# Self-attention's front in a decoder block: the order of its DMAs, its scaling and latent products, and one gather on another engine

## The reference

```python
x = _layernorm(x + ffn0)                                   # per entry of the batch
ct_q  = x @ Wd_q_w + Wd_q_b;  ct_kv = x @ Wd_kv_w + Wd_kv_b    # the latents, 64 wide each
query = heads(ct_q @ Wu_q_w + Wu_q_b) + heads(_rope(ct_q @ Wq_r_w + Wq_r_b, cos, sin))
key   = heads(ct_kv @ Wu_k_w + Wu_k_b) + heads(_rope(x @ Wk_r_w + Wk_r_b, cos, sin))
value = heads(ct_kv @ Wu_v_w + Wu_v_b)                     # 16 heads, 8 wide
attn  = softmax(einsum('bhqd,bhkd->bhqk', query, key) / 12)
out   = einsum('bhqk,bhkd->bhqd', attn, value) @ Wo_w + Wo_b
```

## Time and profile before

| | us |
|---|---|
| median of 3 runs (lowest to highest) | 450.51 (449.87 to 451.18) |
| the profiled execution's own time | 447.8 |
| its span, first to last instruction | 446.0 |
| TensorE busy in the span | 407.5 (91%) |
| VectorE busy | 303.2 (68%) |
| ScalarE busy | 205.1 (46%) |
| GpSimd busy | 196.5 (44%) |
| mean granted clock, as a share of 2.4 GHz | 0.986 |

### The profile page before, as it was taken

How to read it: one execution, slowest core, us unless ns; L and a number is a source line. 1 busy time by engine, 2 the same in 40 slices (tenths; PEclk the granted TensorE clock), 3 DMA queues, 4 the chain that set the end, 5 groups by cost and what they waited for, 6 DMA issues and landing times.

```text
span 446.0 us, 7698 instructions
## 1 busy us (share of the span) xinstructions
PE 407.5 (91%) x2882; PEld 275.8 (62%) x2882; DVE 303.2 (68%) x688; ACT 205.1 (46%) x290; POOL 196.5 (44%) x237
## 2 busy tenths in 40 slices
PE   4898999999999999989999986799779999999985
PEld 4576644455555557747898764445555555558974
DVE  4779976768988888624424978573798894355654
ACT  1676633154333333242333476457256545557550
POOL 3316657699988887050322556212453233000000
PEclk9989999999999999999999998899999999999999
DMA  8812000000005111350251015100000000010000
GB/s 299 320 33 85 2 1 1 1 1 0 1 0 190 48 47 48 100 193 1 103 77 22 2 31 69 15 3 3 0 2 3 2 3 2 2 37 1 0 1 24
DMA packets 8080, 19.78 MB, mean 44 GB/s; under 512 B 1958, under 2 KB 3974, under 8 KB 7526
## 3 DMA queue, kind: packets, MB, share of 16 engines
q1 hardware_dynamic: 8044, 19.30, 14.6%
HBM read 17.26 MB, written 1.15 MB: 41 GB/s over the span
## 4 chain that ended last, share of the span: by engine, by line
PE 72%; DVE 14%; DMA 5%; issue 3%; POOL 3%; ACT 3%; SPq 0%; DVEq 0%; POOLq 0%; ACTq 0%
PE ps L1676 70%; DMA late<-mid 4%; DVE ps L1421 3%; DVE big L1227 2%; DVE ps L1222 2%; DVE mx_a L1425 1%; PE ps L1688 1%; DMA ident<-in_ident 1%; DVE big L1298 1%; POOL rstd L638 1%; POOL big L657 1%; PE ps L2150 1%; PE ps L2073 0%; ACT late L1073 0%; DVE mid L1451 0%
## 5 line engine op out<-in xcount | busy, mean ns | idle before, releaser
L1676 PE MATMUL ps<-big,late 128*32 128x256 f32 (+3 forms) x768 | 96.1, 380 | 3.2 <-DVE mx_a L1425 1.5
L967 ACT ACTIVATE big<-ps 128x1024 f32<-128x1024 f32 x48 | 49.0, 1023 | 39.5 <-PE ps L1676 39.3
L1676 PE MATMUL ps<-late,big 128*128 128x128 f32 (+1 forms) x448 | 65.6, 277 | 1.5 <-DMA late<-mid 1.5
L1676 PEld LDWEIGHTS ps<-big,late 128*32 128x32 f32 (+2 forms) x768 | 36.7, 116 | 38.1 <-issue 14.9
L1676 PEld LDWEIGHTS ps<-late,big 128*128 128x128 f32 (+1 forms) x448 | 47.2, 152 | 19.7 <-issue 12.9
L636 POOL TENSOR_SCALAR vareps<-meanvar 128x2 f32<-128x2 f32 (+2 forms) x13 | 2.9, 226 | 110.0 <-DVE meanvar L1121 106.2
L907 ACT ACTIVATE big<-ps 128x1024 f32<-128x1024 f32 x32 | 31.0, 1022 | 38.9 <-PE ps L1676 37.5
L1421 DVE CUSTOM_DVE_ANT_0 ps<-ps,big 128x512 f32<-128x512 f32 x64 | 42.7, 708 | 6.9 <-PE ps L1676 5.8
L703 POOL TENSOR_TENSOR big<-big 128x512 f32<-128x512 f32 x31 | 43.8, 1428 | 5.5 <-DVE big L1298 5.3
L1298 DVE TENSOR_SCALAR big<-big 128x1024 f32<-128x1024 f32 x32 | 36.4, 1159 | 13.2 <-ACT big L907 12.8
L929 ACT ACTIVATE big<-ps 128x512 f32<-128x512 f32 x32 | 19.1, 597 | 36.7 <-PE ps L1676 36.7
(11 more groups left out here) (261 smaller groups left out, 754.4 us busy)
## 6 DMA issues: line engine op xcount, KB each, us to landing
attn_w<-in_w_x SPq DMA_DIRECT2D x1, 2560.0 KB, 13.6
big<-parts_kx SPq DMA_DIRECT2D x18, 128.0 KB
late<-in_w_up SPq DMA_DIRECT2D x1, 2048.0 KB, 7.8
late<-in_w_dn SPq DMA_DIRECT2D x4, 512.0 KB, 3.8
attn_w<-in_w_up SPq DMA_DIRECT2D x1, 1024.0 KB, 7.9
attn_w<-in_w_dn SPq DMA_DIRECT2D x1, 1024.0 KB, 10.1
big<-mid SPq DMA_DIRECT2D x24, 32.0 KB, 1.8
parts_kx<-ctx_r SPq DMA_DIRECT2D x1, 768.0 KB, 3.2
```

The costliest lines, as they stand in the source:

```text
L967: nc.scalar.activation(ex1[:, n % 3, :].rearrange("p (r n) -> p r n", r=2), ps[:, 2 * (n % 2):2 * (n % 2) + 2, :], ACT.Exp, scale=scale).t ...
L1676: return nc.tensor.matmul(o, lhsT, rhs, start=start, stop=stop, skip_group_check=shared)
```

## The change

It edits only the order and the place of instructions.

- One query gather, `("qa", 1, 1)`, moves from GpSimd to VectorE, which does it right behind its gather `("qa", 1, 0)`.
- `stack_x` can issue some of its pieces. SP now issues the maxima of group 0 first, then six pieces of half 0, the maxima of group 1, two pieces, the maxima of group 2, the last piece with the ones, and the maxima of group 3.
- ScalarE copies entry 1's latents ahead of the evacuation of spread 7 instead of behind it.
- VectorE scales entry 1 behind the first row's maximum instead of the second, and adds the values' bias between the gathers and row 8's maximum instead of behind row 15's.
- TensorE transposes entry 1 behind row 2 instead of row 3, makes its products behind row 3 and spread 6 instead of row 6, and its latent products ahead of the first transpose of maxima instead of behind it. The values' product moves from the end of the front to ahead of the spreads 8 to 12, of which 12 now stands ahead of row 8. Spreads 13, 14 and 15 follow rows 9, 11 and 13.
- The first logits no longer wait for the last transposed maxima and for all spreads; these two waits now stand behind the first logits and ahead of the second.

```diff
             "act": [("ka", 0, 0), ("ka", 1, 0)],
-            "dve": [("qa", 0, 0), ("qa", 0, 1), ("qa", 1, 0), ("qx", 0, 0), ("qx", 1, 0)],
+            "dve": [("qa", 0, 0), ("qa", 0, 1), ("qa", 1, 0), ("qa", 1, 1), ("qx", 0, 0), ("qx", 1, 0)],
...
-            stack_x(sp, 0)
-            for k in range(groups("a")):
-                spread_max("a", k)
+            spread_max("a", 0)
+            stack_x(sp, 0, range(0, 6))
+            spread_max("a", 1)
+            stack_x(sp, 0, range(6, 8))
+            spread_max("a", 2)
+            stack_x(sp, 0, range(8, PARTS * PARTS))
+            spread_max("a", 3)
...
-            for f in (1, 2, 3):
+            for f in (2, 3):
                 gather_four("qa", 1, f)
             minus_parts("a", 1)
...
+                front_latent(1)
                 spread(7)
-                front_latent(1)
                 minus_max("a", 0, dict(first_banks("a"))["max", 0])
...
                     row_max("a", i, bank)
-                    if i == 1:
+                    if i == 0:
                         front_scaled(1)
                     if i == 7:
                         rotated(1, "k")
                         rotated(1, "q")
                         gather_four("qa", 1, 0)
-                dve.wait_ge(S["va_ps"], 1)
...
+                        gather_four("qa", 1, 1)
+                        dve.wait_ge(S["va_ps"], 1)
...
                 for slot, bank in slots_beside("a", None):
+                    if slot == ("max", 0):
+                        latent_products(1)
                     if slot == ("row", 8):
                         idle_work(2, 8)
-                        for n in (8, 9, 10, 11):
+                        values_a()
+                        for n in (8, 9, 10, 11, 12):
                             spread_a(n)
...
+                    if slot == ("row", 2):
+                        front_cols(1)
                     if slot == ("row", 3):
-                        front_cols(1)
                         spread_a(6)
+                        front_products(1)
                     if slot == ("row", 5):
                         spread_a(7)
-                    if slot == ("row", 6):
-                        front_products(1)
-                    if slot == ("max", 0):
-                        latent_products(1)
                     if slot in (("row", 9), ("row", 11), ("row", 13)):
-                        spread_a(12 + (slot[1] - 9) // 2)
-                spread_a(15)
-                values_a()
-                for slot, bank in slots_beside("a", None)[-2:]:
-                    used("a", slot)
+                        spread_a(13 + (slot[1] - 9) // 2)
                 pe.wait_ge(S["va_done"], 1)
+                used("a", first_in("a", (1,)))
+                logits("a", 0)
+                used("a", first_in("a", (2,)))
                 pe.wait_ge(S["a_spread"], len(SPREADS))
-                logits("a", 0)
```

More of the change, by code:

```diff
@@ L520, in program, with stack_x @@
         block = ctx.enter_context(nc.Block())
-        def stack_x(sp, half):
+        def stack_x(sp, half, pieces=range(PARTS * PARTS)):
             heads = slice(HB * half, HB * half + HB)
             sp.wait_ge(S[f"x_zero{half}"], 2 - half)
-            for c in range(PARTS * PARTS):
+            for c in pieces:
                 sp.dma_start(ks["x"][DH * c:DH * c + DH, heads, :],
@@ L529, in stack_x @@
                              .rearrange("(h d) t -> d h t", d=DH)).then_inc(S["x_stack"], 16)
-            sp.dma_start(ks["x"][STACK:ROWS, heads, :], ones_rows[:, heads, :]
-                         ).then_inc(S["x_stack"], 16)
+            if PARTS * PARTS - 1 in pieces:
+                sp.dma_start(ks["x"][STACK:ROWS, heads, :], ones_rows[:, heads, :]
+                             ).then_inc(S["x_stack"], 16)
         @block.sync
@@ L1477, in attend_a @@
                         gather_four("qa", 1, 0)
-                dve.wait_ge(S["va_ps"], 1)
[L1479 to L1483, removed]
+                        gather_four("qa", 1, 1)
+                        dve.wait_ge(S["va_ps"], 1)
+                        dve.wait_ge(S["ones"], 2)
+                        nc.vector.tensor_tensor(
+                            values_of("a"), ps[:, 0, :].rearrange("p (j h d) -> p j h d", j=NJ, h=H),
+                            rv4("Wu_v_b").rearrange("p j (h d) -> p j h d", h=H), ALU.add
+                        ).then_inc(S["va_done"], 1)
                 for n in range(B * (H // 4) * KEYS["a"] // P):
```

## The result

The changed kernel takes 447.61 us (median of 20 runs, 444.64 to 452.19), the kernel before 450.04 us on the same occasion (20 runs, 447.66 to 453.95): a ratio of 0.9932, 95% interval 0.9910 to 0.9954, 3.1 us less (2.1 to 4.1). Forecast were 447.7 us and 2.8 us less. The two medians differ by 2.4 us only, since the ratio leaves out, as slow, the four runs of the changed kernel of 451.5 us and more and none of the kernel before. A later set of 12 runs, beside 35 of the kernel before, gave 0.9988 (0.9955 to 1.0021). With every run counted, the mean gain was 2.0 us in the first set and 1.1 in the later one. A straight line of time over mean granted clock, laid through all 32 runs of the changed kernel and 105 of the kernel before, puts the changed kernel 1.5 us lower at the same clock (1.1 to 1.8). That is about half of the forecast; the experiments say why.

What follows compares the result with a forecast made beforehand. A chain over engines, with transpose, spread, values and bias behind the last row maximum, was taken as the bound, not the transfer. The terms gave 3.0 us at the chain, 2.6 at the first exponential; taking 2.8, 450.5 - 2.8 = 447.7 us, range 445.8 to 449.8.

Steps and rivals of the forecast that it cites:

- part 5: Behind the second transpose of maxima: logits follow directly at full clock, 1.95 us from last maximum to row 16's.
- part 4: Rows 8 to 15: five spreads instead of four precede row 8; the eight maxima and second transpose come 0.6 us later.
- The transfer costs 0.3 us: Ahead of the first logits: the 15.91 us transfer of the first group's maxima delays them by only 0.3 us.
- Part 1: Entry 1's front before row 8: row 7's maximum 0.45 us later, earlier latents cancel it, rotations end within 0.1 us.
- Part 2: Query gather on VectorE: three copies of 0.41 us each, finished at 275.15, covered by the wait for row 8.
- Part 3: Values ahead of rows 8 to 15: product (1.2 us) and bias (0.69 us) leave the end of the front, product free.
- Part 6: SP's reordered queue: second group's maxima land 2.5 us before the fifth logits; effect 0, a loss the only other end.
- The 2.7 us between the profiled execution and the median: Whole kernel: the median of runs lies 2.7 us above the profiled time, unexplained, taken as untouched by the change.
- (a): At the first logits: the low clock stays, leaving a gain of 1.9 us, 448.6 us; chance 0.17.
- (b): Front: stays as long as before, low clock over rows 8 to 15, 1 us gain left, 449.5 us; chance 0.12.
- (c): SP's queue: without a profile pieces run slower, so removing the late first landing is worth more, 446 us; chance 0.12.
- (d): SP's queue: second group's maxima land late behind six slow pieces, 451.9 us and more; chance 0.07 with similar waits.

Runs made afterwards that it cites:

- e1: The kernel before with only SP's new order of transfers and maxima issues; ratio 1.0012 (0.9988 to 1.0036) to the kernel before.
- e3: The changed kernel with entry 1's scaling, transposes, products, latent products and latents' copy back where they were; ratio 0.9943 to the kernel before.
- e4: The changed kernel with the query gather (qa, 1, 1) back on GpSimd; ratio 0.9946 to the kernel before.
- e2: The changed kernel with SP's old order, all ten transfers of half 0 ahead of the maxima; ratio 0.9969 to the kernel before.
- e12: The changed kernel with SP's old order, the same program as e2 once more; ratio 0.9958 to the kernel before.
- e7: The changed kernel with all ten transfers of half 0 between the maxima of group 0 and group 1; ratio 0.9959 to the kernel before.
- e8: The changed kernel with each of the first six pieces followed by an unread 128 KB transfer to spare HBM; ratio 0.9964 to the kernel before.
- e9: The kernel before with SP's new order, values' product and bias ahead of row 8, spread 12 behind it, first logits before the last two waits; ratio 0.9952.
- e10: Kernel e9 with idle matmuls added behind the values' product and behind spreads 9 and 10; ratio 0.9939 to the kernel before.
- e5: The changed kernel with the gather (qa, 1, 1) on GpSimd and spread 12 behind row 8; ratio 0.9954 to the kernel before.

## Why the prediction was right, and where it was not

The mechanism was right: what hung behind the last row maximum was the gain, and the long transfer was not. The closeness of 447.61 to the forecast 447.7 is partly luck. The forecast starts from 450.5 where the kernel before took 450.04 on the occasion, and the gain at the same clock is 1.5 us over all runs, not 2.8. The difference lies mainly in part 5 (1.0 us) and part 4 (0.5 us).

- *The transfer costs 0.3 us, the rest hides behind it.* Right: e1 removes it and gains nothing.
- *Part 1, the front cancels.* Row 7's maximum 0.37 us later (forecast 0.45), VectorE idle 1.25 us ahead of row 4 (1.3), first transpose of maxima 0.9 later (0.8), first spread of entry 1 0.14 later (within 0.1). In e3 the first three are back at the values of before and so is that spread.
- *Part 2, the gather is hidden.* Six copies took 2.58 us (forecast 2.44), and e4 shows that the three of them are as well off on GpSimd. The Trainium skill's rule of the port pair that VectorE and GpSimd share (SBUF — State Buffer, under SBUF: two separate sides) speaks for copies of the slow kind here; the trace agrees with 0.43 us each beside a working GpSimd, and it made no time, since VectorE waited anyway. The factor of two that the prediction reads from the earlier trace rows is not one between alone and beside: the timelines of both engines show the copies of 215 ns too beside a copy of GpSimd, for 120 ns of it. They are the first of their series; the next took 340 ns and the later ones 420 to 447. So no run here shows what a copy takes alone.
- *Part 3, the values are free.* At 269.44 and 277.37 they lie in gaps, as forecast.
- *Part 4, row 8 0.9 us later.* It came 1.3 later, and the second transpose 1.06 instead of 0.6. The term was under-sized because I carried over one low stretch of 3.4 us in the front; the execution had 6.8. (Also, eight maxima at 0.61 us from 276.25 end at 281.2, not at 281.35; the eight took 5.12 us, as the larger figure has it.) With 3.4 us, in e3, row 8's maximum started at 18.2 and T is 23.7, where 18.3 and 23.6 were forecast; the rotations of e3 ended 0.14 us earlier, the rest of the difference goes with the clock.
- *Part 5, 1.95 us from the last maximum to row 16's.* It is 1.86 (283.71 to 285.57). The gap to the first logits is 0.21 us, the clock there 1.00. This step was right in mechanism and in size, but I booked as the change's gain what is partly the luck of one profile: 0.84 us of the 2.60 lie between L and R, and e1 got 1.0 us there without touching the engines. Set against e1 (R at 27.4, low clock 6.8 us in both fronts) the change gives 1.6 us, set against the kernel before 2.6. The timed gains, 3.1 and 0.5 us, lie around these, and the 1.5 us at the same clock agree with the value against e1. This is where the forecast is too large: it took away a low stretch of the earlier trace rows, worth 1.0 us, as if the wait of 1.13 us had to bring it. Of the two profiles with a wait there one had it, and e1, with a wait of 0.94 us, had not. That the low clock falls on the logits less often when they start without a wait is not shown.
- *Part 6, SP's order costs nothing.* Right (R to the end unchanged). Group 1's maxima landed at 288.90 and the fifth logits began at 291.28: 2.4 us of cover, 2.5 forecast. The price of the pieces was set too low: six took 11.1 us by the forecast and 12.0 here, 9.9 in e3; in the kernel before the last of the ten had landed at 283.3, not 281. That the new order's own worth is zero in both profiles without it, e2 and e12, I had not forecast; I had held the landing at 283.8 to be fixed.
- *The 2.7 us between the profiled execution and the median* go with the clock, which I had not found. The profiled execution had a mean clock of 0.986. Of the 105 runs of the kernel before, the 18 at 0.986 or 0.987 have a median of 448.0 us and the 45 at 0.979 or 0.980 one of 450.8; the last section has more.
- *Rivals.* (a), the low clock at the logits, did not come in any of the 13 other profiles. (b), the low clock running on over rows 8 to 15 with T 2 us later, did not come in the changed kernel's two profiles (T 1.06 later), but in e4, e7 and e12 it did: 10.2 us of low clock and T 2.0 to 2.1 us later, which is 283 on the clock of before. There R is still 1.6 us ahead of before, not 1. (c) is out on the mean: if the first landing were late in many executions, e1 would gain, and its ratio is 1.0012 (0.9988 to 1.0036). (d) did not come: 2.0 to 2.4 us of cover in the changed kernel, e7 and e8.

## What to carry to other kernels

The longest item of the chain of waits is worth only what the next releaser leaves: a transfer of 15.91 us was worth 0.3 by the rows and nothing that could be told when it was removed, and what had to move was the small serial tail (a product of 1.2 us, a bias of 0.7) that stood behind the last row maximum though nothing in it depended on that. Look for work that an in-order list puts behind the critical result, and move it into a wait that exists already; the edits of e9 carried the gain here, and of these SP's order was not needed; the other moves carried none. When run-to-run spread is as large as the effect, measure stages between two landmarks within a profile, compare only stages with the same granted clock, and don't book a low stretch of one profile as something that the change takes away.

## What the runs showed of the hardware

The spread of this kernel's runs goes with the mean granted clock: of the 20 runs of the changed kernel, those at 0.976 took 450.3 to 452.2 us and those at 0.990 444.6 to 447.3. Within the profiles the low clock lay at other places in other executions: 0 to 10.2 us of it in the front, stretches of 3.4 us elsewhere. All 14 profiles have one in the last 5 us of the span. From cross-attention's first row maximum to the end the span takes 126.7 us in the seven profiles that have no other there, 128.2 in the five with one more, and 129.8 in the two with two more: 1.5 us each. The two in e10 (same columns as above):

```profile
317.90:321.40 3.50, 3.37 (x13) 2.58 (x13) 1.64 (x5) 0.98 (x2) 2.10 (x4) 0.51 0.02 5
328.10:331.60 3.50, 3.28 (x16) 2.43 (x15) 2.53 (x8) 1.53 (x4) 3.08 (x7) 0.52 0.00 1
```

The one at 194 cost about 2 us, by the start of row 0's maximum in the six profiles with it and the eight without. Between row 16's maximum and cross-attention's first the time was 33.07 us within 0.01 in twelve of fourteen profiles (33.7 and 33.8 in e3 and e5). So a difference of 1.5 to 2 us between two profiled spans of this kernel says nothing until these stretches are counted. The rate of one kind of transfer also varied. The nine pieces and the rows of ones in the same order of SP, from the first packet to the last, in the kernel before and in e2:

```profile
263.60:282.10 18.50, 12.90 (x83) 8.79 (x83) 14.33 (x28) 10.74 (x14) 9.62 (x22) 0.91 0.50 68
```

```profile
262.90:279.70 16.80, 13.94 (x82) 9.11 (x83) 15.60 (x31) 11.30 (x14) 8.46 (x19) 0.80 0.49 75
```

In e12, the program of e2 again, it was 69 GB/s, and six pieces went at 66 in the changed kernel and at 80 in e3.
